# Expert layer on one Trainium2 core: up products woven, down result picked, up activations stored output column first

## What is computed

```python
def kmoe(x_flat, W_router, A, B, scale, bias, d_in1, d_in2, d_out1, d_out2, top_k):
    logits = x_flat @ W_router.T
    vals, idx = jax.lax.top_k(logits, top_k)
    probs = jax.nn.softmax(vals, axis=-1)
    xs = x_flat.reshape(-1, d_in1, d_in2)
    Ag = A[idx]
    Bg = B[idx]
    Y = jnp.einsum('nkoi,nij,nkpj->nkop', Ag, xs, Bg)
    out = jnp.einsum('nkop,nk->nop', Y, probs).reshape(-1, d_out1 * d_out2)
    return out * scale + bias
h = kmoe(x_flat, W_up, A_up, B_up, scale_up, bias_up, 32, 32, 64, 64, 2)
h = jax.nn.gelu(h, approximate=False)
y = kmoe(h, W_down, A_down, B_down, scale_down, bias_down, 64, 64, 32, 32, 2)
x = x + layernorm(y)
```

## Time and profile before

| what | value |
|---|---|
| runs | 869.92, 874.09, 874.47 us; median 874.09 |
| profiled execution | 870.78 us, of which the traced span is 868.8 |
| PE busy | 654.9 us, 75% of the span |
| up products | 342.0 to 387.2 us |
| down logits | 390.8 to 409.5 us |
| down products | 434.7 to 482.7 us |

### The profile page before, as it was taken

How to read it: one execution, slowest core, us unless ns; L and a number is a source line. 1 busy time by engine, 2 the same in 40 slices (tenths; PEclk the granted TensorE clock), 3 DMA queues, 4 the chain that set the end, 5 groups by cost and what they waited for, 6 DMA issues and landing times. The chain is left out here.

```text
span 868.8 us, 18294 instructions
## 1 busy us (share of the span) xinstructions
PE 654.9 (75%) x7522; PEld 386.0 (44%) x7554; DVE 519.9 (60%) x1094; ACT 344.7 (40%) x522; POOL 358.8 (41%) x330
## 2 busy tenths in 40 slices
PE   0627878788786389868875478248998988999995
PEld 0313444444444389758765324123333344444442
DVE  8656666676664633221502668878999984415265
ACT  1422444334443653330423463246554535434320
POOL 9202444444442300000001062328998983966530
PEclk9968999999998579878868599659999998999999
DMA  3156540000000632200000470000000000000000
GB/s 76 36 120 150 68 66 0 0 0 0 0 1 1 223 85 49 53 3 2 2 5 5 136 235 0 0 0 1 0 1 0 0 1 1 1 0 1 12 13 24
DMA packets 17326, 29.75 MB, mean 34 GB/s; under 512 B 3248, under 2 KB 13168, under 8 KB 16240
## 3 DMA queue, kind: packets, MB, share of 16 engines
q1 hardware_dynamic: 17264, 28.87, 13.1%
HBM read 24.54 MB, written 4.19 MB: 33 GB/s over the span
## 5 line engine op out<-in xcount | busy, mean ns | idle before, releaser
L474 ACT ACTIVATE pr_exp<-at_psum 128x1024 f32<-128x1024 f32 x68 | 69.6, 1024 | 128.2 <-PE at_psum L559 128.2
L366 DVE TENSOR_REDUCE pr_neg_max<-at_psum 128x4 f32<-128x1024 f32 x68 | 83.2, 1225 | 49.7 <-PE at_psum L541 49.7
L316 POOL TENSOR_SCALAR_AFFINE_SELECT pr_exp<-pr_exp 128x512 f32<-128x512 f32 x68 | 47.1, 692 | 155.6 <-ACT pr_exp L474 155.6
L1481 POOL TENSOR_TENSOR all_phi_b<-all_phi_b,mo_work 128x512 f32<-128x512 f32 x56 | 71.0, 1268 | 44.6 <-ACT mo_work L1687 40.0
L749 POOL TENSOR_TENSOR all_x<-all_x,ff_x_blocks 128x512 f32<-128x512 f32 x3 | 3.8, 1267 | 187.5 <-ACT ff_x_blocks L933 187.5
L1502 PE MATMUL all_psum<-all_phi,mo_xt 128*128 128x512 f32 x128 | 66.3, 645 | 7.4 <-ACT mo_work L1669 5.6
L1451 POOL TENSOR_TENSOR mo_work<-mo_work,mo_max 128x1024 f32<-128x1024 f32 x32 | 61.4, 1918 | 21.5 <-DVE mo_max L1743 21.5
L536 PE MATMUL at_psum<-band_mask,all_ident_bf 128*128 128x512 bf16 x104 | 35.7, 401 | 40.9 <-DVE pr_q_window L359 27.6
L1535 PE MATMUL all_psum<-mo_xt,all_phi_centred 128*128 128x512 f32 x128 | 66.3, 598 | 0.0
L1588 PE MATMUL all_psum<-mo_work,mo_y_slots 128*128 128x512 f32 x128 | 62.5, 595 | 1.8 <-DVE mo_work L1791 1.8
L1687 ACT ACTIVATE mo_work<-all_psum 128x512 f32<-128x512 f32 x64 | 37.7, 601 | 61.9 <-PE all_psum L1535 61.9
(11 more groups left out here) (339 smaller groups left out, 1335.6 us busy)
## 6 DMA issues: line engine op xcount, KB each, us to landing
all_expert_w<-in_expert_w SPq DMA_DIRECT2D x1, 4096.0 KB, 18.2
ff_b_up<-in_b_up SPq DMA_DIRECT2D x1, 2048.0 KB, 9.1
ff_a_up<-in_a_up SPq DMA_DIRECT2D x1, 2048.0 KB, 14.0
ff_w_down<-in_w_down SPq DMA_DIRECT2D x2, 1024.0 KB, 20.7
at_q_stack<-parts_scratch SPq DMA_DIRECT2D x24, 64.0 KB
at_k_stack<-parts_scratch SPq DMA_DIRECT2D x24, 64.0 KB
at_q_stack<-parts_scratch SPq DMA_DIRECT2D x12, 128.0 KB
at_k_stack<-parts_scratch SPq DMA_DIRECT2D x12, 128.0 KB
```

Of the source, the lines that this page charges most:

```text
L316: nc.gpsimd.affine_select(out=e[:, g, :, 0, :], in_=e[:, g, :, 0, :], compare_op=ALU.is_ge, fill=0.0, base=0, pattern=[[0, GH], [-1, P]], ...
L366: nc.vector.tensor_reduce(negm[:, GH * g:GH * g + GH].rearrange("p (u r) -> p r u", r=2), psum[:, SN + 2 * (g % 2):SN + 2 * (g % 2) + 2, : ...
L474: nc.scalar.activation(e[:, g, :, :, :].rearrange("p h j q -> p (h j q)"), psum[:, ST:ST + 2, :].rearrange("p b n -> p (b n)"), ACT.Exp).t ...
L1481: nc.gpsimd.tensor_tensor(tot[:, ch % 2, :], first, ec[:, ch % 2, j, :], ALU.add).then_inc(added, 1)
```

## The change

`h` becomes `[P, F1, N]`: the column outside, the token inside. DVE now writes single elements 512 bytes apart, Gelu takes 32 columns by 32 tokens, a logits matmul streams 128 adjacent elements, and `first_down` loads its 64 stationary elements 512 bytes apart. The up products are woven: after a quarter of `second(j)` comes one `first(f)` of four matmuls. In the down products the two experts of a token stay apart: `second_down` is one 64x64 by 64 matmul that makes all four combinations of the two experts' factors; `rows_out`, now a matmul against half an identity (`pick`), keeps the two wanted ones and adds them in PSUM, on top of a bias that a 512-column matmul (`row_of`, `bias_down`) puts there first. ACT and DVE each copy one of the two banks of v and one of the two of y, per chunk.

```diff
-        h = a.sb("h", [P, N, F1])
+        h = a.sb("h", [P, F1, N])
...
+        yb = x4[:, NT:2 * NT, :].rearrange("p g n -> p (g n)").rearrange("p (u k n w a) -> p u k n w a", u=2, k=K, n=8, w=2)
...
-                        v.scalar_tensor_tensor(out=h[:, 32 * j + r:32 * j + 32:4, :], in0=psum[:, h_bank(4 * j + r), :].rearrange("p (g o) -> p g o", o=F1),
+                        v.scalar_tensor_tensor(out=h[:, :, 32 * j + r:32 * j + 32:4].rearrange("p o g -> p g o"), in0=psum[:, h_bank(4 * j + r), :].rearrange("p (g o) -> p g o", o=F1),
...
-                def take_y(gr):
-                    dve.wait_ge(y_done, 2 * gr + 2)
-                    if gr >= 2:
-                        dve.wait_ge(nat_done, gr - 1)
-                    for w in range(2):
-                        v.scalar_tensor_tensor(out=yb[:, gr % 2, :, w, :], in0=psum[:, w, 0:8 * D1].rearrange("p (n a) -> p n a", n=8), scalar=scales[:, 1:2],
-                                               in1=bias_dn[:, :].unsqueeze(1).broadcast_to([P, 8, D1]), op0=ALU.mult, op1=ALU.add).then_inc(y_ready, 1)
+                def take_v(ch):
+                    dve.wait_ge(v_done, ch + 1)
+                    if ch >= 4:
+                        dve.wait_ge(y_done, ch - 3)
+                    v.tensor_copy(vs[:, ch % 4, 1, :, :, :].rearrange("p n k b -> p (n k b)"), psum[:, v_bank(ch) + 1, :]).then_inc(v_dve, 1)
+
+                def take_y(ch):
+                    dve.wait_ge(y_done, ch + 1)
+                    if ch >= 2:
+                        dve.wait_ge(nat_done, ch - 1)
+                    v.tensor_scalar(yb[:, ch % 2, :, :, 1, :], psum[:, 1, :].rearrange("p (n k a) -> p k n a", n=8, k=K), scales[:, 1:2], None, ALU.mult).then_inc(y_dve, 1)
...
-                        part = h[:, 32 * j + 16 * k:32 * j + 16 * k + 16, :].rearrange("p n o -> p (n o)")
-                        s.activation(part, part, ACT.Gelu).then_inc(gelu_done, 1)
...
+                def gelu(n):
+                    act.wait_ge(hb_ready, 4 * (n // 2) + 4)
+                    rows = h[:, 32 * (n % 2):32 * (n % 2) + 32, 32 * (n // 2):32 * (n // 2) + 32]
+                    s.activation(rows, rows, ACT.Gelu).then_inc(gelu_done, 1)
+
+                for f in range(4):
+                    take_z(f)
+                for n in range(2 * NB):
+                    if n < 2 * NB - 2:
+                        take_z(2 * n + 4)
+                        take_z(2 * n + 5)
+                    if n % 2 == 1 and n >= 3:
+                        gelu(n - 3)
+                        gelu(n - 2)
+                gelu(2 * NB - 2)
+                gelu(2 * NB - 1)
...
+                def second(j, pair, part):
+                    q = 4 * j + 2 * pair
+                    if part == 0:
+                        pe.wait_ge(z_ready, 4 * j + 4)
+                        if q >= 6:
+                            pe.wait_ge(hb_ready, q - 4)
+                    for g2 in range(4 * part, 4 * part + 4):
+                        for k in range(K):
+                            for s in range(2):
+                                for r in (2 * pair, 2 * pair + 1):
+                                    rows = slice(32 * r, 32 * r + 32)
+                                    last = t_.matmul(psum[64 * s:64 * s + 64, h_bank(4 * j + r), F1 * g2:F1 * g2 + F1], z[rows, j % 2, 2 * g2 + s, k, :],
+                                                     ga_up[rows, 16 * j + 2 * g2 + s, k, :], start=(k == 0), stop=(k == K - 1))
+                    if part == 1:
                         last.then_inc(h_done, 1)
...
-                    if j + 1 < NB:
-                        first(j + 1)
-                    second(j)
+                    for pair in range(2):
+                        for part in range(2):
+                            second(j, pair, part)
+                            if j + 1 < NB:
+                                first(4 * j + 4 + 2 * pair + part)
...
-                        last = t_.matmul(psum[col:col + 64, s, 0:N], wdn[rows, o, :], h[rows, :, o], start=(o < 2), stop=(o >= F1 - 2))
+                        last = t_.matmul(psum[col:col + 64, s, 0:N], wdn[rows, o, :], h[rows, o, :], start=(o < 2), stop=(o >= F1 - 2))
...
-                                last = t_.matmul(psum[64 * w:64 * w + 64, v_bank(ch) + s, 64 * n2:64 * n2 + 64], h[rows, n, :],
+                                last = t_.matmul(psum[64 * w:64 * w + 64, v_bank(ch) + s, 64 * n2:64 * n2 + 64], h[rows, :, n],
...
                     for nn in range(4):
                         for s in range(2):
                             idx = 4 * (nn // 2) + 2 * s + nn % 2
-                            for k in range(K):
-                                for tl in range(2):
-                                    for w in range(2):
-                                        rows, col, n2 = slice(64 * w, 64 * w + 64), 32 * (2 * (ch % 2) + tl), 4 * tl + nn
-                                        last = t_.matmul(psum[col:col + 32, w, D1 * idx:D1 * idx + D1], vs[rows, ch % 4, s, n2, k, :],
-                                                         ga_dn[rows, 64 * s + 8 * ch + n2, k, :], start=(k == 0), stop=(k == K - 1))
+                            for tl in range(2):
+                                for w in range(2):
+                                    rows, n2 = slice(64 * w, 64 * w + 64), 4 * tl + nn
+                                    last = t_.matmul(psum[64 * tl:64 * tl + 64, w, 64 * idx:64 * idx + 64], vs[rows, ch % 4, s, n2, :, :].rearrange("p k b -> p (k b)"),
+                                                     ga_dn[rows, 64 * s + 8 * ch + n2, :, :].rearrange("p k a -> p (k a)"), start=True, stop=True)
                     last.then_inc(y_done, 1)
 
-                def rows_out(gr):
-                    pe.wait_ge(y_ready, 2 * gr + 2)
-                    if gr >= 2:
-                        pe.wait_ge(ln_y.by_act, 4 * (gr - 1))
+                def rows_out(ch):
+                    gr = ch // 2
                     out = psum[:, nat_bank(gr), :].rearrange("p (c q b) -> p q c b", c=4, q=4)
-                    src = yb[:, gr % 2, :, :, :].rearrange("p n w (r q) -> p q (n w r)", q=4)
-                    for q in range(4):
-                        last = t_.transpose(out[:, q], src[:, q], c["ident"][:, :])
+                    pick = c["ident"][:, :].rearrange("p (c k b) -> p k c b", c=2, k=K)
+                    if ch % 2 == 0:
+                        if gr >= 2:
+                            pe.wait_ge(ln_y.by_act, 4 * (gr - 1))
+                        t_.matmul(psum[:, nat_bank(gr), :].rearrange("p (c n) -> p c n", c=4), row_of[:, :], bias_dn[:, :].unsqueeze(1).broadcast_to([R, 4, P]), start=True, stop=False)
+                    pe.wait_ge(y_act, ch + 1)
+                    pe.wait_ge(y_dve, ch + 1)
+                    for k in range(K):
+                        src = yb[:, ch % 2, k].rearrange("p n w (r q) -> p q (n w r)", q=4)
+                        for q in range(4):
+                            last = t_.matmul(out[:, q, 2 * (ch % 2):2 * (ch % 2) + 2, :], src[:, q], pick[:, k], start=False, stop=(ch % 2 == 1 and k == K - 1 and q == 3))
...
-                    if ch >= 2 and ch % 2 == 0:
-                        rows_out(ch // 2 - 1)
-                rows_out(3)
+                    if ch >= 1:
+                        rows_out(ch - 1)
+                rows_out(NCH - 1)
```

More of the change, by code:

```diff
@@ L925, in take_v, with take_y @@
                         act.wait_ge(y_done, ch - 3)
[L926 to L927 removed]
+                    s.copy(vs[:, ch % 4, 0, :, :, :].rearrange("p n k b -> p (n k b)"), psum[:, v_bank(ch), :]).then_inc(v_act, 1)
+                def take_y(ch):
+                    act.wait_ge(y_done, ch + 1)
+                    if ch >= 2:
+                        act.wait_ge(nat_done, ch - 1)
+                    s.activation(yb[:, ch % 2, :, :, 0, :], psum[:, 0, :].rearrange("p (n k a) -> p k n a", n=8, k=K), ACT.Copy, scale=scales[:, 1:2]).then_inc(y_act, 1)
                 def norm_y(gr):
[L930 removed]
                     act.wait_ge(ln_y.factors, gr + 1)
@@ L934, in norm_y @@
                                      bias=ln_y.tmp[:, 1, t:t + 1], scale=ln_y.tmp[:, 6, t:t + 1]).then_inc(ln_y.by_act, 1)
-                for ch in range(6):
-                    take_v(ch)
-                norm_y(0)
-                take_v(6)
-                take_v(7)
-                for gr in range(1, 4):
-                    norm_y(gr)
+                take_v(0)
+                take_v(1)
+                for ch in range(NCH):
+                    take_y(ch)
+                    if ch + 2 < NCH:
+                        take_v(ch + 2)
+                    if ch >= 3 and ch % 2 == 1:
+                        ln_y.root(act, 2 * ch - 6, 2 * ch - 2, ch // 2 - 1)
+                    if ch >= 4 and ch % 2 == 0:
+                        norm_y(ch // 2 - 2)
+                norm_y(2)
+                ln_y.root(act, 12, NT, 3)
+                norm_y(3)
             @block.tensor
```

(18 more changed lines are left out.)

78 lines of the change are left out of this document (33 added, 45 removed).

## The result

The changed kernel takes **902.34 us** (median of four runs, 895.02 to 905.89), the kernel before 873.13 in the same comparison: a ratio of **1.033, interval 1.026 to 1.040**. Slower by 3.3%, where faster by 1.7% was forecast. Where runs of a kernel lie over 1.5% above its fastest (three of twelve in one experiment), its ratio leaves them out. The profiled execution took 905.9 us, its span is 904.2, against 868.8 before: 35.4 us more.

What follows compares the result with a forecast made beforehand. PE was taken as the bound, standing still for blocks of code at 27 ns per record. Terms -8.6, -9.4, +2.8 and +0.1 gave -15.1 us: 855.7 for the profiled execution, 859 forecast, range 848 to 873.

Steps and rivals of the forecast that it cites:

- Up products, forecast 36.6 us: Up products: the woven order takes 36.6 us against 45.2, a change of -8.6 us.
- so no pauses here: Woven up products: 72 records in 2.02 us, 28 ns each, just slower than code arriving at 27, hence no pauses.
- a granted clock of 0.5 through the woven part: Rival, woven up products: the clock stays low, +16 us, so 875; chance 9%.
- 3.4 us a piece: Woven up products, low-clock rival: price of one piece with `first` at 207 and `second` at 27 ns per record.
- Logits, forecast -9.4: Logits: 256 records go from 73 to 36 ns each, all put on the distance of streamed elements, -9.4 us.
- the adding up in PSUM: Rival, logits: this, not distance, slows them; +9.4 there, no +9.4 in `first_down`, near 859; no chance given.
- that term: Up products: DVE's scattered writes priced at nothing; if doubled, only the last pair, 0.7 us each, would show.
- `first_down`, 36 ns per record: Down products: 512 records with scattered weight loads at 36 ns, 18.4 us, against 17 ns at full clock before.
- the rival that scattered loads don't overlap: Rival, `first_down`: 110 ns per record, 38 us more, 897; chance 8% serial, 10% partly serial (864 to 870).
- Picking, forecast 16.3 us: Down products: 8 x 16 picking records at the pace of `first`, 124 to 128 ns, 16.3 us.
- the weights lie 16 bytes apart ... free: Picking: this distance costs nothing, from loads of 218 ns at L1093 against 215 for contiguous L950.
- Down stage, code: Down products: pauses are code fetch; 1160 records, 31 us of fetch, fit under PE's 51; rival "not code", 875, 5%.

Runs made afterwards that it cites:

- the fine weave: Kernel before with only the up products woven, 64 records of `second` then 8 of `first`: ratio 1.015, 890.47 us; the changed kernel has the same order.
- the coarse one: Kernel before with only the up products woven, in pieces twice as long (128 records of `second`, then 16 of `first`): ratio 0.999, 876.15 us.
- the first experiment: Kernel before with only the storage of `h` changed to column outside, up products not woven, down products as before: ratio 0.994, 870.96 us.

## Why the prediction was wrong

It is off by 50.2 us in the profiled execution (905.9 against a sum of 855.7). By its own steps:

- **Up products, forecast 36.6 us, measured 60.4: +23.8.** The step that failed is "so no pauses here". I derived pauses only from how fast PE asks for code, 28 ns per record against 27. I had quoted the stage's 3 us gap within the 6.2 us of issue gaps and never asked when it comes: behind the 2 MB load. It comes with that load in whatever order PE works, 3.04 us in the kernel before, 3.31 with the new `h`, 3.29 and 3.40 in the fine weave, 3.93 in the coarse one, and it goes, or shrinks to 1.11 in the old order, when the load goes. The second half is the clock. It was a rival with a chance of 9%, "a granted clock of 0.5 through the woven part", and my argument against it was that the pauses go. Its price was too low as well: 3.4 us a piece, from 27 and 207 ns per record, where 3.92 was measured; the row of 207 ns is from a stretch that was only partly at half clock, as the pieces after it show (8 records in 2.01 us, 251 ns). Without the load the rest of the step was right: no pause in the woven part, and 38.7 us, not 36.6.
- **Logits, forecast -9.4: right.** 9.62 us instead of 18.66, 8.66 in the kernel with the storage alone. It was the distance, not the adding up in PSUM. Gelu's wait grew from 3.65 to 4.22 us, 0.6 more. DVE's scattered writes, which lie before it, take 0.34 us longer each, 1087 ns against 747; I had put that term at nothing from two copies of 692 and 688 ns, and those didn't stand for it.
- **`first_down`, 36 ns per record: right**, 20.5 us busy instead of 18.4. The rival that scattered loads don't overlap fell: the loads take 244 ns each on the mean and come 38 ns apart, so they do overlap at 512 bytes. `second_down` 14.2 instead of 12.3 (most of its steps ran at 1.99 us for 64 records, 31 ns, where I took 24) and bias 5.4 instead of 3.8 (1.12 or 2.07 us for two records); the busy times of neighbours overlap by 2.6 us.
- **Picking, forecast 16.3 us, measured 31.7: +15.4.** The step that failed is "the weights lie 16 bytes apart ... free", from transposes with loads of 218 ns against 215. I never looked at the clock under those two rows. Both ran at the lower level; these are the stretches of L950 (contiguous) and of the first four of L1093 (16 bytes apart) in the kernel before, the granted clock ahead of the DMA share:

```profile
295.00:299.20 4.20, 3.57 (x16) 3.00 (x16) 2.89 (x16) 3.51 (x9) 0.00 (x0) 0.52 1.00 429
454.40:455.50 1.10, 1.10 (x12) 0.77 (x12) 0.00 (x0) 0.98 (x2) 0.00 (x0) 0.50 0.00 0
```

At that clock the distance costs little in the picking too, 246 ns per record against 225 adjacent. At full clock it costs 126: 246 against 120. The loads of transposes show the same, with a smaller price. In the first experiment the loads of L1093, 16 bytes apart, take 208 ns at a granted clock of 1.00 (447.4 to 448.1), and contiguous loads at 1.00 in the kernel before (712.9 to 715.1) take 141:

```profile
L1540 PEld LDWEIGHTS all_psum<-all_ident,all_phi 128*128 128x128 f32 x16 | 1.8, 141 | 0.9 <-issue 0.5 <-DVE all_phi L1770 0.2
```

Of the 15.4 us, 11.6 went when the elements became adjacent; the 3.8 that remained over 16.3 are pickings at the lower clock, 3.5 to 3.7 us instead of 2.0. The pace of 127 ns that I took for the picking was one of the full clock, and the "free" one of the half clock. A row that would have warned was L958, 219 ns per scattered load, which I used only for the rival on `first_down`. The Trainium skill ("SBUF — State Buffer", the note on cachelines) has four fp32 as the free stride; for the weights of a matmul the measurement differs, 246 ns against 120 at full clock, from a change of the distance alone.
- **Down stage, code.** That the pauses there are code, and go with fewer records, was right: 0.32 us is left, and the wait of 3.98 us for `y_block` is gone. The saving was real, and the new work cost more.

Together: +23.8 in the up products and +18.4 in the down products (69.2 against 50.8), of which picking is 15.4; +0.9 at Gelu and logits; +0.3 at routing and gather; the layers before and after, where only the 0.1 us of `row_of` had been forecast, +7.1. That is 50.5 in the span, 50.2 by device time. The +7.1 has no cause here: the layer before is the same code and ended anywhere in a stretch of 7.2 us in these executions.

That the Trainium skill ("Runtime: NRT & Kernel Launch", Instruction fetch mechanics) calls the fetch hidden is contradicted further: a block of code behind 2 MB of loads cost 3.0 to 3.9 us, and more through the clock.

Left open: what lowers the clock after one pause or wait and not after another as long, and what brings it back, so why one weave recovers and the other doesn't; and whether DVE's slower writes cause the longer `z` waits of the storage-only kernel.

## What to carry to other kernels

A bulk load that no engine waits for can still stop an engine that runs on much code: look in the DMA view for the gap between code packets, and start such loads one piece at a time. Moving the whole load only moved the pause, to the logits here; a place with little code was not tried. A stall of 3 us can cost 20 if the clock falls with it and doesn't come back (60.4 us against 38.7 here), so price a stage at both clocks before relying on one. Before calling a stride free, compare rows at the full clock: here the same 16 bytes cost 21 ns at half clock and 126 at full.

## What the runs showed that was not expected

- Matmul weights 128x128 in fp32: 16 bytes apart 246 ns per record at either clock; adjacent 120 ns at full clock and 225 at half. Scattered, the granted clock makes no difference; adjacent, the full clock nearly halves the time.
- Loads of 64 elements 512 bytes apart in four packed tiles: 37 to 39 ns per record, both at a granted clock of 1.00 (446.37) and at a mean of 0.56 (465.27 in the changed kernel), against 17 ns adjacent at full clock and 31 at half. Here too the clock makes no difference once the load is scattered.
- During 2 MB of back-to-back transfers (10 us) in the changed kernel no code packet is seen before the very end: one in 16 us, where three came in the same 16 us without the load. One 512 KB transfer at a time let code through, at most with a pause of 2.33 us.
- DVE writes of single fp32 elements 512 bytes apart cost 1087 ns for 512 columns, against 747.
- A granted clock of 0.5 can follow waits of the same length or not: after 2.62 us in one kernel, not after 2.61 us at the same point of another.
